# Moving the mixed blocks of a routed expert stage closer together, and four small loads from SyncE to GpSimd

## What is computed

```
h   = layernorm(x)
phi = elu(.) + 1
q, k, v = h Wq' + bq, h Wk' + bk, h Wv' + bv        (16 heads of 16)
x1  = x + ((phi(q) * cumsum(phi(k) * v)) / 4) Wo' + bo
n   = layernorm(x1)
top two of 8 experts from n @ router_w, softmax over the two
out = x1 + sum over the two of score * (silu(n w1g[e]) * (n w1u[e])) w2[e]
         + (silu(n w_gate) * (n w_up)) w_down
```

## Time and profile before

| | us |
|---|---|
| median of three executions | 387.16 |
| lowest, highest | 384.04, 387.60 |
| the profiled execution, its own time | 390.16 |
| its span in the profile | 388.4 |
| TensorE busy | 339.3 (87%) |
| VectorE busy | 235.6 (61%) |
| ScalarE busy | 213.9 (55%) |
| GpSimd busy | 172.3 (44%) |

### The profile page before, as it was taken

How to read it: one execution, slowest core, us unless ns; L and a number is a source line. 1 busy time by engine, 2 the same in 40 slices (tenths; PEclk the granted TensorE clock), 3 DMA queues, 4 the chain that set the end, 5 groups by cost and what they waited for, 6 DMA issues and landing times. The chain is left out here.

```text
span 388.4 us, 9002 instructions
## 1 busy us (share of the span) xinstructions
PE 339.3 (87%) x2867; PEld 253.1 (65%) x2867; DVE 235.6 (61%) x578; ACT 213.9 (55%) x385; POOL 172.3 (44%) x269
## 2 busy tenths in 40 slices
PE   6967488979988898986999898999999999999930
PEld 5756377868877787875888554566556656655620
DVE  5889957667686686786678654445444544553410
ACT  4678627658577685774526444554554545545420
POOL 4723185467575666515230212334343363444353
PEclk9899699989999999999999999999999999999995
DMA  6965232256473454715755636866894775686440
GB/s 201 378 167 192 45 95 84 57 117 184 91 231 90 111 192 99 169 63 149 234 161 178 110 70 100 92 72 95 99 91 71 117 104 88 86 110 84 55 47 1
DMA packets 77852, 46.42 MB, mean 119 GB/s; under 512 B 61424, under 2 KB 72944, under 8 KB 77424
## 3 DMA queue, kind: packets, MB, share of 16 engines
q1 hardware_dynamic: 63664, 35.09, 37.8%
q0 software_dynamic: 9472, 10.70, 17.5%
q10 hardware_dynamic: 4672, 0.07, 1.1%
HBM read 19.09 MB, written 12.97 MB: 83 GB/s over the span
## 5 line engine op out<-in xcount | busy, mean ns | idle before, releaser
L1395 DVE SCALAR_TENSOR_TENSOR ab<-bU,sg 128x512 f32<-128x512 f32 x64 | 44.1, 689 | 67.3 <-PE bU L949 48.6
L714 POOL DMA_INDIRECT out_y<-xs,dst_row x32 | 50.9, 1592 | 69.1 <-issue 27.0
L1078 ACT ACTIVATE sg<-bG 128x512 f32<-128x512 f32 x64 | 37.9, 592 | 47.2 <-PE bG L949 22.6
L949 PE MATMUL bG<-we,work 128*128 (+1 forms) x216 | 52.6, 380 | 0.8 <-DVE wd L1451 0.6
L949 PE MATMUL bU<-we,work 128*128 (+1 forms) x216 | 52.6, 379 | 0.0
L564 POOL DMA_INDIRECT x_rows<-rows,slot_u x32 | 35.7, 1116 | 28.2 <-DVE slot_u L1446 10.9
L1222 ACT ACTIVATE ws_h<-ab 128x512 f16<-128x512 f32 x36 | 22.7, 629 | 40.4 <-DVE ab L1395 35.9
L1671 DVE TENSOR_TENSOR ws_h<-ab,ws_h 128x512 f16<-128x512 f32 x36 | 24.9, 693 | 20.7 <-ACT ws_h L1222 19.5
L1400 DVE TENSOR_TENSOR al<-ab,ah 128x512 f16<-128x512 f32 x32 | 22.1, 690 | 23.1 <-ACT ah L1085 22.9
L949 PEld LDWEIGHTS bG<-we,work 128*128 128x128 f16 (+1 forms) x216 | 20.9, 99 | 20.3 <-issue 3.1
L233 PE MATMUL bG<-xT,ws_h 128*128 128x256 f16 x160 | 28.2, 280 | 5.4 <-ACT sg L1078 2.7
(11 more groups left out here) (285 smaller groups left out, 795.9 us busy)
## 6 DMA issues: line engine op xcount, KB each, us to landing
stage<-in_w_expert SPq DMA_DIRECT2D x24, 512.0 KB
we<-in_w_shared SPq DMA_DIRECT2D x3, 1024.0 KB, 10.3
xs<-bo POOLq DMA_DIRECT2D x8, 256.0 KB, 3.9
out_y<-xs SPq DMA_DIRECT2D x8, 256.0 KB, 2.2
xs<-in_x SPq DMA_DIRECT2D x1, 1280.0 KB, 18.2
x_rows<-we SPq DMA_DIRECT2D x9, 134.0 KB
xs<-in_x SPq DMA_DIRECT2D x3, 256.0 KB, 4.5
work<-x_rows SPq DMA_TRANSPOSE x40
```

Source lines behind the costliest of these rows:

```text
L714: pool.indirect_dma_start(out_rows, bass.IndirectOffsetOnAxis(ap=dst_row[:, b:b + 1], axis=0), ya[b % NY], None, bounds_check=NT * P - 1, ...
L949: ins = pe.matmul(dst[t * n:(t + 1) * n, :], x2[:, hi * KC + k, t * n:(t + 1) * n], w[t][lo][:, k, half, :], start=s == 0 and k == 0, stop ...
L1078: act.activation(sg[q][:], src[:], ACT.Silu, scale=1.0 / WS).then_inc(S["sg_done"], 1)
L1395: dve.scalar_tensor_tensor(out=ab[q][:], in0=src[:], scalar=1.0 / WS, in1=sg[q][:], op0=ALU.mult, op1=ALU.mult).then_inc(S["a_done"], 1)
```

## The change

`GAP` goes from 8 to 6, so that the mixed blocks are at 5, 11, 17 and 23. Constants that depend on it follow; one more constant keeps unused half slots away from the positions, and the copies of the second expert's weights are spread over four blocks in place of five. The small loads of blocks 0 to 3 are no longer issued by SyncE but by GpSimd, before the masks, with a semaphore for each; the small loads of later blocks count on semaphores of their own too, so that TensorE's wait for a block's rows no longer includes them.

```diff
-    GAP = 8
+    GAP = 6
-    N_CONST = 31
+    N_CONST = 32
...
         def rows_in(b):
-            return S[f"xg_in{b % NX}"], sum(64 if n in MIXED else 32 for n in range(b % NX, b + 1, NX))
+            return S[f"xg_in{b % NX}"], sum(32 if n in MIXED else 16 for n in range(b % NX, b + 1, NX))
+
+        def meta_in(b):
+            if b < NX:
+                return S[f"first_meta{b}"], 16
+            return S[f"meta_in{b % NX}"], sum(32 if n in MIXED else 16 for n in range(b % NX + NX, b + 1, NX))
...
-                    if b < NX:
-                        sp.dma_start(meta[t * n:(t + 1) * n, b, :], src[:, 2 * D:2 * D + 8]).then_inc(got, 16)
...
+                    const(pool.tensor_scalar(at_slot[:, 2:3], row_f[:], float(HALF + NPAIR), float(P), ALU.is_ge, ALU.mult))
...
-                    const(pool.tensor_tensor(slot_w[:, 1, 0:1], at_slot[:, 1:2], row_f[:], ALU.add))
+                    const(pool.tensor_scalar(slot_w[:, 1, 0:1], at_slot[:, 1:2], row_f[:], at_slot[:, 2:3], ALU.add, ALU.add))
...
+            meta_reg = pool.alloc_register("meta_reg")
+            pool.wait_ge(S["row_done"], 1)
+            for i in (B - 2, B - 1):
+                saved, n = saved_before(i + 2)
+                pool.wait_ge(saved, n)
+            pool.wait_ge(S["padded"], 16 * (E + 1))
+            pool.nop(nofuse=True)
+            for b in range(NX):
+                pool.reg_load(meta_reg, blk_row[b:b + 1, :])
+                at = pool.snap(meta_reg, min_val=0, max_val=E * CAP)
+                pool.dma_start(meta[:, b, :], xrows[bass.ds(at, P), 2 * D:2 * D + 8]).then_inc(S[f"first_meta{b}"], 16)
 
             pool.wait_ge(S["spread_out"], 2)
...
                     act.dma_start(meta[t * n:(t + 1) * n, b, :], xrows[bass.ds(at, n), 2 * D:2 * D + 8]
-                                  ).then_inc(S[f"xg_in{b % NX}"], 16)
+                                  ).then_inc(S[f"meta_in{b % NX}"], 16)
...
                 if k == 0:
-                    dve.wait_ge(*rows_in(b))
+                    dve.wait_ge(*meta_in(b))
...
-                    if MIXED[q] - 5 <= b < MIXED[q]:
-                        for k in ((0,), (1,), (2,), (3,), (4, 5))[b - MIXED[q] + 5]:
+                    if MIXED[q] - 4 <= b < MIXED[q]:
+                        for k in ((0,), (1,), (2, 3), (4, 5))[b - MIXED[q] + 4]:
                             lend_weights(q, k)
```

More of the change, by code:

```diff
@@ L219, in layer_kernel @@
             rt pt slot_const spread_in spread_ps spread_out end_done padded bexp_done pad_done
-            xg_in0 xg_in1 xg_in2 xg_in3 sign_done score_done dst_done ta_ps ath_done atl_in0 atl_in1 atl_in2 o_ps y_done hold_done row_done lent tl_ps atl_last halves_out scattered0 scattered1""".split()
+            xg_in0 xg_in1 xg_in2 xg_in3 first_meta0 first_meta1 first_meta2 first_meta3 meta_in0 meta_in1 meta_in2 meta_in3 sign_done score_done dst_done ta_ps ath_done atl_in0 atl_in1 atl_in2 o_ps y_done hold_done row_done lent tl_ps atl_last halves_out scattered0 scattered1""".split()
         S = {n: sem(n) for n in names}
```

## The result

Over eight executions of each on one chip the changed kernel takes 389.28 us in the median (387.87 to 391.33), the kernel before 386.08 (383.98 to 387.60): a ratio of 1.0089, interval [1.0053, 1.0124], or 3.4 us slower. The forecast was 5.4 us slower, 392.6 (388.5 to 396.5).

A forecast was written before the change was run, and what follows sets the result against it. The prediction took GpSimd's chain of scatters, each waiting for an earlier landing, to set the end. Profiled 390.16 + 5.4 (positions) + 0 (small loads) = 395.6, less 3.0 to the median: 392.6 us, range 388.5 to 396.5.

The forecast's parts named there:

- a chain that catches up: End of the routed stage: the last scatter would follow its result, at 374.6 in place of 380.97, 6.4 us less.
- The count of steps: GpSimd's scatters, block 5 to 35: from 14 full waits, 8 E, 12 S to 16 full waits, 7 E, 11 S.
- The term of 5.4 us: Moving the mixed blocks to 5, 11, 17, 23 adds one landing to the scatter chain: 131.87 us against 126.41.
- mean landing of 5.41: Average full wait in GpSimd's scatter chain, from issue through landing to the next issue, used to size the steps.
- E and S steps: S: scatter finding its condition met, 1.86 us; E: the next, waiting for the scatter two back, full wait minus S.
- Nothing: Small loads leaving SyncE bring rows and saves forward but gain 0 us, as TensorE waits for VectorE's cast.
- bound of 1.4 us: Stage start: most that GpSimd's four added small loads could cost by delaying the masks; taken as 0.
- A backlog cleared early: Rival, 8%: after the last mixed block at 23 the scatter chain catches up with TensorE; faster, 380.8 us.
- Landings get shorter: Rival, 17%: scatter landings average near the break-even of 5.17 us, so no change, 387.2 us.
- bound of 8.7: Late routed stage: ScalarE waiting for landings makes TensorE end at most 8.7 us later, still ahead of the last scatter.
- the bubbles: TensorE's waits, in which its clock might fall: upper bound 2 us; rival with GpSimd late at the start, 394.6, 12%.

The follow-up runs named there:

- noadd8: base8 with the scatters' bound on row numbers at 0, so nearly no row is added though every scatter is still issued and waited for: 0.9877 of the kernel before.
- joined8: base8 where halves of a mixed block belonging to one expert no longer wait for each other; waits remain where the expert changes: 0.9901 of the kernel before.
- eight_buffers6: base6 with eight result buffers in place of four, so ScalarE's result of a block needs the landing eight blocks back: 1.0111 of the kernel before.
- base6: The changed kernel with one more register operation, a lower bound of 16 on the value a scatter waits for: 1.0110 of the kernel before.
- gap_only: base8 with GAP = 6, its constants and the four-step weight copies; small loads stay on SyncE with shared semaphores: 1.0067 of the kernel before.
- base8: The kernel before with one more register operation, a lower bound of 16 on the value a scatter waits for: 1.0015 of the kernel before.
- loads_only: base6 with GAP = 8 and five-step weight copies, so small loads on GpSimd with their own semaphores remain: 1.0034 of the kernel before.

## Why the prediction was right, and where its sizes were off

**The bound.** Right. Shorter landings (noadd8) or fewer of them (joined8) take 1.0 to 1.2% off the kernel before, 3.8 to 4.7 us of the 6.4 that the prediction had put on a chain that catches up; freeing TensorE alone (eight_buffers6) gives nothing.

**The count of steps.** Right in the four profiles with mixed blocks at 5, 11, 17 and 23 and the old waits (after, base6, gap_only, eight_buffers6): full waits at 9, 13, 22, 27 and 29 besides the mixed blocks, short pairs between. Only in the profile after are the last steps, to blocks 31 to 35, more even, 2.3 to 3.3 us each.

**The size of the positions' cost.** The term of 5.4 us was too large. The chain lasts 126.41, 126.07 and 126.39 us with GAP 8, and 128.00, 129.04, 131.36 and 129.50 with GAP 6: 129.5 - 126.3 = 3.2 us more. The mean landing of 5.41, used for all steps alike, was the error. The two added steps cost 10.4 us (three expert changes take 16.8 us on average with GAP 8, five take 27.1 with GAP 6), but the E and S steps fell by 6.9 us (52.9 to 46.0), where I took off one of each, 5.41. About 1 us of that is the last step: with GAP 6 block 35 is an E step and takes 2.4 to 2.8 us, where the other E steps average 3.7 (block 34 before it holds only padding, which may be why; no run tests it). For the rest, some of the short steps had not been short before, as block 25's 3.68 (342.54 - 338.86). In time, the positions cost 0.5 to 0.8%, 2.0 to 2.9 us (gap_only over base8, base6 over loads_only).

**The small loads.** Costed at 0, and this was wrong. The step that failed is the "Nothing" behind "TensorE's wait at the stage's start is for VectorE's last cast of weights, 0.6 us, not for rows", and the same for the separate semaphores. GpSimd was not late, as the masks' stamp shows, so the bound of 1.4 us priced the wrong path; the loss is 1.7 us on average over four comparisons (0.2, 0.4, 0.5 and 0.65%). Of it 0.3 us lies behind the last scatter, 0.5 on average in the wait for block 2's turn, if the small loads cause it, and the rest has no row. The Trainium skill's rule that plain transfers belong on SyncE's or ScalarE's queues pointed the right way; but GpSimd's time per issue, 0.53 to 0.60 us against SyncE's 0.41, doesn't explain the loss.

Two terms were off in opposite directions, 5.4 for 2 to 3 and 0 for 1.7: that the sum, 5.4 for 3.4, was nearer than its first term is luck.

**The range and the chances.** The range of 388.5 to 396.5 is about half a us wider at each end than the 3.5 us that it was worked out from; the measured 389.28 lies in either, near the lower end. The chances put 0.72 on over 1% slower and 0.20 on within 1%, and the measured 0.9% falls in the second. The 1% that the prediction took for the least a measurement can tell was too coarse: the interval here is 0.35% either way.

**The rivals.** A backlog cleared early did not happen: mean landings stayed at 5.2 to 5.4. The rule of about 2.0 us plus bytes / 436e3 from the Trainium skill, "DMA: Bandwidth & Descriptors", section "Anatomy of one DMA", agrees with its fixed part alone: with nearly no rows added a half's step is 3.45 us, 1.9 beside the issue of 1.55. With the rows added full steps behind a whole block average 5.0 to 5.8 us in the trace, where the prediction's estimate from that page was 3.9. "Landings get shorter" was in part the case, one profile's 5.24. TensorE ended later, by 3 to 5 us: its last product starts 121.2 us behind block 5's first scatter after the change and 123.1 in base6, against 118.0 in base8 (368.47 - 250.48). That is within the bound of 8.7 and, as forecast, ahead of the last scatter. Its clock didn't fall in the bubbles: the granted clock was 1.00 from 340 to 372 us in the profiles of the changed kernel and of base6.

**The better version.** joined8 (0.9901 and 0.9903) keeps the positions of before and the small loads on SyncE: 381.45 us in the median where the kernel before took 385.85.

## What to carry to other kernels

An engine that is 87% busy need not set the end: follow the last instruction back, and if it is a chain of DMAs that wait for each other, count landings, not bytes. Moving a costly step to a place where it hides nothing can add steps elsewhere; here expert changes that had been free under a mixed block became full waits, and the cure was to drop waits that the data does not need. A releaser that a view names is only the last event before the start: compare it with when that work was done. Size such a change by the mean of each kind of step, and give an edit that moves DMAs between queues a run of its own, even where no listed wait belongs to it.

## What the runs showed of the hardware

A scatter that adds 128 rows of 1 KB takes 5.0 to 5.8 us from its issue to the next dependent issue, by the means of each kind of step in the seven profiles with the old waits and all rows added. From a first half, with 64 rows, to the second it is 4.7 to 4.9 us on average and was 3.45 us with nearly no row added, so some 70% of it doesn't come from the rows. Two such scatters in flight overlap well: a second one about 1.9 us behind the first is followed 3.4 to 3.8 us later by the next, so the pair takes 5.4 to 5.7 us on average, hardly more than one. Four 16-byte-per-row loads from GpSimd take 0.53 to 0.60 us each at issue, under half of its 256 KB load.
